# Attention beside a gated ternary feed-forward: the second score pass shifted by maximum plus logarithm of the sum, the first pass by groups of heads, contexts in two banks

## Chip, cores and metric

One Trainium2 chip, one core. The metric is the device time of one execution in microseconds, median of the runs. The engines are TensorE (PE), VectorE (DVE), ScalarE (ACT), GpSimd (POOL) and SyncE (SP), which here only issues DMAs.

## The reference

For each of 8 sequences of 512 tokens with 512 features:

```
xn = layernorm(x)
q, k, v = xn @ Wq.T, xn @ Wk.T, xn @ Wv.T      # 16 heads of 32, rope on q and k
scores = q k^T / sqrt(32), causal
s = softmax(scores) v, heads joined, @ Wo.T
h = gelu(bitlinear(xn, w_fc))                   # 512 -> 2048, ternary weights, a layernorm ahead
f = bitlinear(h, w_proj)                        # 2048 -> 512, a layernorm ahead
out = x + s * silu(f)
```

## The kernel before

All five engines run one program, written out by hand, with semaphores between them. One pass of `body(b)` handles one sequence; the body of the next one follows directly, and each engine executes its own instructions strictly in the order in which `body` emits them. Activations are split in a high and a low float16 part, so most products are two or three matmuls. The 512 tokens are four tiles of 128 (`NT`), the 16 heads are four groups of four (`NG`, `GH`), the 2048 hidden features are 16 chunks (`FC`).

For one sequence TensorE does, in this order: the value products and the query and key products (L414); the first tile of the output projection of the sequence before; the up projection (L539), 16 chunks, with the first two score rounds between the last chunks; then the **first score pass**; a stretch between the passes; and the **second score pass**, in whose last part it turns the tokens of the next sequence (L445).

**The first score pass** has 44 rounds (`ROUNDS`). A round is a tuple: tile of queries, first head, number of heads. It fills one of five PSUM banks (`S_BANKS`) with scores in which queries lie on partitions (L518), adds the causal mask by a matmul (L525), and then VectorE takes the maximum of each row (L1103), GpSimd turns it into a bias (L1322), and ScalarE takes the exponential with that bias and accumulates the sum of each row (L846). The rounds of the tile 0 have four heads of 128 keys ("short" rounds): there VectorE subtracts the maximum itself (L1111), ScalarE takes one exponential (L838), and VectorE sums, two rounds later (L1117). Before the change the rounds go tile 3 for all heads, tile 2 for all heads, and then four times a short round with two rounds of tile 1. A bank is given to the next round when its row sum is ready. Between the score rounds TensorE executes filler, `downs`: 36 matmuls of the late output projection (L431, tiles 1 to 3) and then the down projection by half tiles (L570, six halves of 32 matmuls, given two by two), and last the fourth tile (L579, 32 matmuls of 512 columns). `GIVEN[r]` says how many items of filler have been issued once round r is out: 20 after round 4, and 115 of 132 after the last round. ScalarE copies four finished halves away (L855), the last two stay in PSUM. VectorE also scales three tiles of output by the gate (L1036), after the rounds in `SCALED_AFTER`.

**Between the passes** VectorE splits the negated maxima in three float16 parts (L1025 to L1028), TensorE turns them (L605), VectorE copies them (L1144), and one DMA puts them into three more rows of the query stack, against three rows of ones in the key stack. TensorE meanwhile does the rest of the down projection and the sums for the second layernorm (L611, L616).

**The second score pass** computes the scores of each head again, with keys on partitions (L638, `scores(h)`), in two regions of PSUM used in turn; ScalarE takes the exponential of the 1280 causal columns (L869); GpSimd zeroes the masked blocks (L1351); and TensorE weighs the values (L669, `weigh(g, j)`), for a group of four heads at a time, while the scores of the next group are made. Everything of a context is in bank 6. The probabilities are not normalised: VectorE inverts the row sums (L1184), splits them (L1025 to L1028 again), TensorE turns them (L647), and for each group a matmul with a selector spreads the inverses over bank 7 (L664), VectorE copies them (L1202) and multiplies the context by them (L1205), ScalarE casts the product to float16 (L860) and GpSimd subtracts for the low part (L1357).

Around it VectorE computes mean and variance of the hidden features, GpSimd the power of -1/2 for it (L1340, `rstd_ready`), and VectorE the scale of the gate from that (L1177). GpSimd does the ten small steps of the next sequence's layernorm (`normalise_steps`, L1264 to L1282) between the passes; SP stores the norm (L308) and spreads it (L315).

## Time and profile before

| | |
|---|---|
| median of three runs | 1156.67 us (1156.52 to 1157.22) |
| profiled execution | 1157.77 us, its span 1156.0 us |
| PE busy | 1116.3 us, 97% of the span |
| DVE busy | 848.7 us, 73% |
| ACT busy | 791.5 us, 68% |
| POOL busy | 541.1 us, 47% |
| mean granted clock of TensorE | 0.999 |

The profile is of one execution. A matmul's duration in it is the time from its start to its end, and consecutive matmuls overlap, so the pace is read from starts: 16 matmuls of 512 columns that take 0.38 us each fill 3.66 us. Times of the trace are us from the start of the span.

### The profile page before, as it was taken

To read this page: it belongs to the slowest core of one execution; us is meant where nothing else is said; L and a number is where in the kernel's file an instruction comes from. 1 tells how busy PE (TensorE), PEld (TensorE's weight loads), DVE (VectorE), ACT (ScalarE), POOL (GpSimd) and SP (SyncE) were. 2 spreads that over 40 slices of the span, in tenths; PEclk is the share of its full clock that TensorE was granted. 3 is DMA by queue.
4 is the path that set the end of the run, shared out by engine and by line. 5 is a ranking of instruction groups with operands and counts; after the bars stand their busy time and mean duration, and the time that the engine had idled before them with its cause. 6 is when DMAs were issued, how large, how long until landed. Compare 5 with 4: busy or idle time off the path is not lost.

```text
span 1156.0 us, 20105 instructions
## 1 busy us (share of the span) xinstructions
PE 1116.3 (97%) x7580; PEld 609.3 (53%) x7580; DVE 848.7 (73%) x1451; ACT 791.5 (68%) x1508; POOL 541.1 (47%) x950
## 2 busy tenths in 40 slices
PE   4989999999999999999999999999999999999997
PEld 3555644448444574446644475445844467444753
DVE  6997867788457885588756886579845888558854
ACT  4787975589735878279772797448883697827974
POOL 2035352473625635275442755257362563527534
PEclk9999999999999999999999999999999999999999
DMA  8491011730109101361016411082011910145111
GB/s 309 156 108 41 1 30 37 93 88 23 30 8 145 49 3 29 44 121 37 4 28 77 88 38 30 1 107 85 11 30 23 142 38 3 28 58 71 37 40 37
DMA packets 52586, 67.31 MB, mean 58 GB/s; under 512 B 9352, under 2 KB 34312, under 8 KB 51976
## 3 DMA queue, kind: packets, MB, share of 16 engines
q1 hardware_dynamic: 52488, 66.02, 30.2%
q8 instruction: 60, 0.98, 0.4%
q14 instruction: 38, 0.31, 0.1%
HBM read 31.98 MB, written 8.40 MB: 35 GB/s over the span
## 4 chain that ended last, share of the span: by engine, by line
PE 83%; ACT 8%; DVE 5%; DMA 2%; issue 1%; SPq 1%; DVEq 0%; ACTq 0%
PE banks L414 21%; PE banks L539 17%; PE banks L570 13%; PE banks L518 5%; PE banks L669 5%; PE banks L638 5%; PE banks L431 5%; PE banks L579 4%; ACT arena L869 4%; PE banks L525 2%; ACT banks L846 1%; PE banks L445 1%; ACT split_buf L792 1%; DMA stacks<-split_buf 1%; PE banks L452 1%
## 5 line engine op out<-in xcount | busy, mean ns | idle before, releaser
L846 ACT ACTIVATE banks<-banks,mix,scl 128x512 f32<-128x512 f32 (+2 forms) x384 | 248.5, 660 | 7.2 <-POOL mix L1322 4.5
L1103 DVE TENSOR_REDUCE mix<-banks 128x1 f32<-128x384 f32 (+3 forms) x352 | 217.2, 637 | 31.0 <-PE banks L525 20.1
L539 PE MATMUL banks<-xT,fcT 128*128 128x512 f16 x1024 | 228.1, 379 | 4.6 <-ACT xh_buf L815 4.4
L570 PE MATMUL banks<-proj_ones,arena 128*128 128x256 f16 (+1 forms) x1536 | 213.3, 273 | 0.0
L869 ACT ACTIVATE arena<-banks,scl 128x1280 f32<-128x1280 f32 x128 | 164.8, 1328 | 65.4 <-PE banks L638 61.9
L1308 POOL TENSOR_TENSOR split_buf<-xr_buf,split_buf 128x512 f16<-128x512 f32 x64 | 74.0, 1177 | 254.0 <-ACT split_buf L792 254.0
L1317 POOL TENSOR_TENSOR xh_buf<-xh_buf 128x512 f32<-128x512 f32 x120 | 152.4, 1270 | 48.2 <-ACT xh_buf L815 40.2
L414 PE MATMUL banks<-xT,qkT 128*128 128x512 f16 x768 | 168.7, 379 | 0.0
L539 PEld LDWEIGHTS banks<-xT,fcT 128*128 128x128 f16 x1024 | 98.5, 98 | 124.3 <-ACT xh_buf L815 9.8
L570 PEld LDWEIGHTS banks<-proj_ones,arena 128*128 128x128 f16 x1536 | 142.6, 97 | 33.8
L1322 POOL TENSOR_SCALAR mix<-mix,scl 128x1 f32<-128x1 f32 (+1 forms) x288 | 75.9, 265 | 150.7 <-DVE mix L1103 150.1
L1076 DVE TENSOR_TENSOR arena<-banks,mix 128x512 f32<-128x512 f32 x128 | 79.5, 683 | 85.0 <-PE banks L414 85.0
L820 ACT ACTIVATE banks<-banks,scl 128x512 f32<-128x512 f32 x128 | 84.8, 663 | 75.4 <-PE banks L539 75.2
L1351 POOL TENSOR_SCALAR_AFFINE_SELECT arena<-arena 128x256 f32<-128x256 f32 x256 | 105.2, 437 | 62.3 <-ACT arena L869 62.1
L518 PE MATMUL banks<-stacks 96*128 96x128 f16 (+3 forms) x512 | 127.7, 300 | 1.5 <-DVE mix L1117 0.6
L414 PEld LDWEIGHTS banks<-xT,qkT 128*128 128x128 f16 x768 | 74.8, 98 | 87.9
L792 ACT CAST split_buf<-xr_buf 128x512 f16<-128x512 f32 x64 | 37.6, 616 | 118.9 <-DVE xr_buf L1082 78.3
L1125 DVE TENSOR_SCALAR arena<-banks,scl 128x512 f16<-128x512 f32 x128 | 96.0, 750 | 29.4 <-ACT banks L820 29.3
L1127 DVE SCALAR_TENSOR_TENSOR arena<-banks,scl,arena 128x512 f16<-128x512 f32 x128 | 96.2, 751 | 4.5
L638 PE MATMUL banks<-stacks 99*128 99x512 f16 (+3 forms) x512 | 91.4, 301 | 5.5 <-ACT arena L869 3.5
L815 ACT ACTIVATE xh_buf<-banks,scl 128x512 f32<-128x512 f32 x128 | 87.2, 681 | 0.5 <-DVE arena L1127 0.4
L669 PE MATMUL banks<-arena,v_sb 128*32 128x512 f32 (+3 forms) x1024 | 87.2, 441 | 0.0
(160 smaller groups left out, 1515.0 us busy)
## 6 DMA issues: line engine op xcount, KB each, us to landing
stacks<-split_buf SPq DMA_DIRECT2D x192, 128.0 KB, 5.1
out_dram<-arena SPq DMA_DIRECT2D x32, 256.0 KB, 2.0
xr_buf<-in_L_attn_x_dram SPq DMA_DIRECT2D x7, 1024.0 KB, 7.6
resid<-in_L_attn_x_dram SPq DMA_DIRECT2D x28, 256.0 KB, 5.3
stacks<-in_L_ffn_w_fc_dram SPq DMA_DIRECT2D x1, 4096.0 KB, 25.3
arena<-in_L_ffn_w_proj_dram SPq DMA_DIRECT2D x1, 4096.0 KB, 14.9
mix<-norm_row SPq DMA_DIRECT2D x8, 256.0 KB, 5.0
xr_buf<-in_L_attn_x_dram SPq DMA_DIRECT2D x4, 256.0 KB, 3.6
```

What stands on the lines that cost most here:

```text
L414: mm = pe.matmul(out_ap, lhs, rhs, start=(c == 0 and k == 0), stop=(c == n - 1 and k == 2))
L518: pe.matmul(bank[:, k * keys:(k + 1) * keys], q_stack[0:KS, h0 + k, i * P:(i + 1) * P], k_stack[0:KS, h0 + k, 0:keys], start=(k == 0), sto ...
L539: mm = pe.matmul(banks[:, UP_BANKS[f % NUB], :], fcT[:, c, f * P:(f + 1) * P], xT[:, part, c, :], start=(c == 0 and part == 0), stop=(c == ...
L570: mm = pe.matmul(banks[:, DOWN_BANKS[h % 3], 0:cols.stop - cols.start], hid[:, part, f, t * P:(t + 1) * P], proj_ones[:, f, cols], start=( ...
L638: mm = pe.matmul(ps[:, at:at + n], k_stack[0:KM, h, j * P:(j + 1) * P], q_stack[0:KM, h, j * P:S], start=True, stop=True)
L669: mm = pe.matmul(banks[k * DK:(k + 1) * DK, 6, j * P:S], v_sb[:, j, head * DK:(head + 1) * DK], probs[:, g % 2, k, at:at + n], start=(j == ...
L846: mm = nc.scalar.activation(block, block, ACT.Exp, scale=col(EXP_SCALE), bias=exp_bias[:, i, h0 + k:h0 + k + 1], accum_out=row_sum[:, i, h ...
L869: nc.scalar.activation(probs[:, g % 2, h % GH, :], st_region[h % 2][:, 0:PROBS], ACT.Exp, scale=col(EXP_SCALE)).then_inc(probs_ready, 1)
L1103: nc.vector.tensor_reduce(row_max[:, i, h0:h0 + n], scores_of(r), AX_X, ALU.max).then_inc(max_ready, 1)
L1127: nc.vector.scalar_tensor_tensor(hid[:, 1, f, :], up, col(INV_G), hid[:, 0, f, :], ALU.mult, ALU.subtract).then_inc(hid_lo_ready, 1)
L1317: nc.gpsimd.tensor_tensor(sq_sum[:], sq_sum[:], squares[f % NSQ], ALU.add).then_inc(sq_added, 1)
L1351: nc.gpsimd.affine_select(blocks, blocks, [[0, 2], [1, P]], ALU.is_ge, 0.0, base=0, channel_multiplier=-1).then_inc(probs_masked, 1)
```

## The change

The softmax of the second pass is normalised by its shift: the rows that are added to the query stack hold maximum + log(sum)/scale (LSE) instead of the negated maximum, against rows of minus ones. So the inversion of the sums, its split, its turn, the spread matmuls, the copies of the spread and the product with it go. The logarithm is made from the bits of the sum (one VectorE instruction), one exponential on ScalarE, and twelve small VectorE instructions. It is made for eight heads at a time: so that the first eight are done early, the rounds of the first pass now go by group of four heads (four rounds of tile 3, the short round, four of tile 2, two of tile 1), and the turned rows reach the query stack in two halves and two DMAs. The first half's logarithm stands on VectorE behind rounds 24 and 27 to 30, its turn on TensorE behind round 34. The banks of the rounds follow a list that is no longer periodic from round 25 on. All six halves of the down projection are given before the end of the rounds (`GIVEN`: 20 after round 4, then 22, 25, 28, 31, 34, ...; 79, 83, 86, 89, 92, 94, 97, 100, 102, 104, 107 after rounds 25 to 35; 132 after the last) and all six are copied away by ScalarE; of the fourth tile's 32 matmuls 16 instead of 12 are issued beside the exponentials of the second pass. Contexts of even groups are in bank 6, of odd ones in bank 7; VectorE copies each out as the high part and subtracts for the low one, without ScalarE or GpSimd. GpSimd's layernorm steps for the next sequence are issued one behind the masks of each head, and the power of -1/2 for the gate behind the masks of head 10.

The core of the diff:

```diff
+HH = H // 2
+LN2 = 0.6931471805599453
+LOG2_CENTRE = 0.0430357
+SCALE_FLOOR = 2.0 ** -7
+GUESS_AFTER = 24
+LSE_AFTER = {27: 0, 28: 1, 29: 2, 30: 3}
+TURN_AFTER = 34
+MAX_COPY_AFTER = 35
 ROPE_SHRINK = 1.0 / 16
 LN_EPS, BIT_EPS = 1e-5, 1e-6
 MASKED = -1e30
@@ -34,16 +42,22 @@
 KEY_COLS = [0, 512, 1024, 896]
 PROBS = 1280
 
-ROUNDS = [(i, h, 1) for i in (3, 2) for h in range(H)]
-ROUNDS += [r for h in range(0, H, 4) for r in ((0, h, 4), (1, h, 2), (1, h + 2, 2))]
+ROUNDS = [r for g in range(0, H, GH) for r in [(3, h, 1) for h in range(g, g + GH)] + [(0, g, GH)]
+          + [(2, h, 1) for h in range(g, g + GH)] + [(1, g, 2), (1, g + 2, 2)]]
...
-S_BANKS = (3, 4, 0, 2, 1)
-NSB = len(S_BANKS)
+NSB = 5
+S_BANKS = 5 * (3, 4, 0, 2, 1) + (3, 0, 4, 2, 1) + (0, 3, 2, 4, 1) + 2 * (0, 2, 3, 4, 1)
...
-LN_EARLY = 6
-IN_BANK_1 = LONG.index(max(r for r in range(NR) if S_BANKS[r % NSB] == 1)) + 1
+RSTD_AFTER_HEAD = 10
...
-    return [lead[r] if r < NSB else lead[-1] + (total - lead[-1]) * EXP_COLS[r - NSB] // EXP_COLS[-1] for r in range(NR)]
+    return [lead[r] if r < NSB else lead[-1] + (total - lead[-1]) * EXP_COLS[r - NSB] // EXP_COLS[-1 - NSB] for r in range(NR)]
...
-DOWN_BESIDE_EXP = 12
+DOWN_BESIDE_EXP = (3, 3, 3, 3, 2, 2)
...
-                sp.wait_ge(maxT_ready, b + 1)
-                sp.dma_start(q_stack[KS:KM, :, :], maxT[:, :]).then_inc(max_dma, 16)
+                for half in range(2):
+                    sp.wait_ge(maxT_ready, 2 * b + half + 1)
+                    sp.dma_start(q_stack[KS:KM, HH * half:HH * (half + 1), :], maxT[:, :]).then_inc(max_dma, 16)
...
+                def turn_lse(half, bank):
+
+                    pe.wait_ge(lse_split, 2 * b + half + 1)
+                    for i in range(NT):
+                        mm = pe.transpose(banks16[0:SPLITS * HH, bank, i * P:(i + 1) * P],
+                                          max_parts[:, half, i].rearrange("p s h -> p (s h)"), ident16[:])
+                    mm.then_inc(maxT_ps, 1)
...
-                while given < ahead + DOWN_BEFORE_MAXIMA:
-                    next(downs)
-                    given += 1
-
-                pe.wait_ge(max_split, b + 1)
-                pe.wait_ge(sum_ready, b * len(LONG) + IN_BANK_1)
-                for i in range(NT):
-                    mm = pe.transpose(banks16[0:SPLITS * H, 1, i * P:(i + 1) * P],
-                                      max_parts[:, i].rearrange("p s h -> p (s h)"), ident16[:])
-                mm.then_inc(maxT_ps, 1)
-
+                    if r == TURN_AFTER:
+                        pe.wait_ge(down_kept, b * N_HALF + turned_in - 2)
+                        turn_lse(0, DOWN_BANKS[turned_in % 3])
+
+                pe.wait_ge(down_kept, b * N_HALF + N_HALF - 1)
...
-                while given < ahead + NT * DOWN_MATMULS - DOWN_BESIDE_EXP:
+                while given < ahead + NT * DOWN_MATMULS - sum(DOWN_BESIDE_EXP):
                     next(downs)
                     given += 1
-
-                pe.wait_ge(sum_ready, b * len(LONG) + len(LONG))
-                pe.wait_ge(short_summed, b * len(SHORT) + len(SHORT))
...
-                    if h == 0:
-                        pe.wait_ge(max_dma, (b + 1) * 16)
+                    if h % HH == 0:
+                        pe.wait_ge(max_dma, b * 32 + 16 * (h // HH) + 16)
+                    if h < 2:
+                        last_in_region = max(q for q in range(NR) if S_BANKS[q] // 3 == h)
+                        pe.wait_ge(sum_ready, b * len(LONG) + LONG.index(last_in_region) + 1)
                     if h == 1:
-                        pe.wait_ge(centred, b * NT + 1)
+                        pe.wait_ge(sums_read, 3 * b + 3)
...
-                            pe.wait_ge(invT_ready, b + 1)
+                            pe.wait_ge(maxT_ready, 2 * b + 2)
+                        elif g == 1:
+                            pe.wait_ge(centred, b * NT + 1)
                         else:
-                            pe.wait_ge(ctx_ready, b * NG + g)
-                    if j == 1:
-                        if g == 0:
-                            pe.wait_ge(centred, b * NT + NT)
-                        pe.matmul(banks[:, 7, :], selector[:, GH * g:GH * (g + 1), :].rearrange("p h d -> p (h d)"), invT,
-                                  start=True, stop=True).then_inc(spread_ps, 1)
+                            pe.wait_ge(ctx_lo, b * NG + g - 1)
                     at, n = KEY_COLS[j], S - j * P
                     for k in range(GH):
                         head = GH * g + k
-                        mm = pe.matmul(banks[k * DK:(k + 1) * DK, 6, j * P:S], v_sb[:, j, head * DK:(head + 1) * DK],
+                        mm = pe.matmul(banks[k * DK:(k + 1) * DK, 6 + g % 2, j * P:S], v_sb[:, j, head * DK:(head + 1) * DK],
...
-                        for _ in range(DOWN_PER_HEAD if g == 0 else 0):
-                            next(downs, None)
-                        if g == 0 and k == GH - 1:
-                            turn_inverses()
+                        for _ in range(sum(DOWN_BESIDE_EXP[GH * g + k:GH * g + k + 1])):
+                            next(downs)
+                        if g == 1 and k == 0:
+                            pe.wait_ge(sums_read, 3 * b + 3)
+                            turn_lse(1, 6)
...
+                def exp_of_guess(half):
+
+                    act.wait_ge(ln_guessed, 2 * b + half + 1)
+                    nc.scalar.activation(exp_guess[:], ln_guess[:], ACT.Exp, scale=-1.0).then_inc(guess_exp, 1)
...
+            def guess_of_lse(b, half):
+                heads = slice(HH * half, HH * (half + 1))
+                dve.wait_ge(sum_ready, b * len(LONG) + len(LONG) // 2 * (half + 1))
+                dve.wait_ge(short_summed, b * len(SHORT) + len(SHORT) // 2 * (half + 1))
+                dve.wait_ge(lse_split, 2 * b + half)
+                nc.vector.tensor_scalar(ln_guess[:], row_sum[:, :, heads].bitcast(I32), LN2 / 2 ** 23, (LOG2_CENTRE - 127) * LN2,
+                                        ALU.mult, ALU.add).then_inc(ln_guessed, 1)
+            def lse_from_guess(b, half):
+                heads = slice(HH * half, HH * (half + 1))
+                parts = max_parts[:, half]
+                one_more, rest = exp_guess, ln_rest
 
                 def step(k, ins):
+                    ins.then_inc(lse_step, 1)
+                    dve.wait_ge(lse_step, (2 * b + half) * 11 + k)
+                dve.wait_ge(guess_exp, 2 * b + half + 1)
+                step(1, nc.vector.tensor_tensor(one_more[:], exp_guess[:], row_sum[:, :, heads], ALU.mult))
+                step(2, nc.vector.tensor_scalar(one_more[:], one_more[:], -1.0, None, ALU.add))
+                step(3, nc.vector.tensor_scalar(rest[:], one_more[:], -0.25, 1.0 / 3, ALU.mult, ALU.add))
+                yield
+                step(4, nc.vector.tensor_tensor(rest[:], rest[:], one_more[:], ALU.mult))
+                step(5, nc.vector.scalar_tensor_tensor(rest[:], rest[:], -0.5, one_more[:], ALU.add, ALU.mult))
+                step(6, nc.vector.scalar_tensor_tensor(rest[:], rest[:], 1.0, one_more[:], ALU.add, ALU.mult))
+                yield
+                step(7, nc.vector.tensor_tensor(rest[:], rest[:], ln_guess[:], ALU.add))
+                step(8, nc.vector.scalar_tensor_tensor(parts[:, :, 0, :], rest[:], col(INV_EXP), row_max[:, :, heads], ALU.mult, ALU.add))
+                step(9, nc.vector.tensor_tensor(part_rest[:], row_max[:, :, heads], parts[:, :, 0, :], ALU.subtract))
+                yield
+                step(10, nc.vector.scalar_tensor_tensor(part_rest[:], rest[:], col(INV_EXP), part_rest[:], ALU.mult, ALU.add))
+                step(11, nc.vector.tensor_copy(parts[:, :, 1, :], part_rest[:]))
+                nc.vector.tensor_tensor(parts[:, :, 2, :], part_rest[:], parts[:, :, 1, :], ALU.subtract).then_inc(lse_split, 1)
+                yield
+            def keep_turned_lse(b, half):
+                dve.wait_ge(max_dma, b * 32 + 16 * half)
+                dve.wait_ge(maxT_ps, 2 * b + half + 1)
+                bank = 6 if half else DOWN_BANKS[((FIRST_GIVEN[TURN_AFTER] if b == 0 else GIVEN[TURN_AFTER] - OUT_BESIDE_SCORES) + FC - 1) // FC % 3]
+                nc.vector.tensor_copy(maxT[:, :], banks16[0:SPLITS * HH, bank, 0:S]).then_inc(maxT_ready, 1)
...
+                first_half = lse_from_guess(b, 0)
                 for r in range(EARLY, NR):
                     maxima(r)
+                    if r == GUESS_AFTER:
+                        guess_of_lse(b, 0)
+                    if r in LSE_AFTER:
+                        next(first_half)
+                    if r == MAX_COPY_AFTER:
+                        keep_turned_lse(b, 0)
                     if r in SCALED_AFTER and not first:
                         scale_by_gate(b - 1, b * 8 + 8, (SCALED_AFTER[r],))
-                dve.wait_ge(max_ready, b * NR + NR)
-                split_parts(max_parts, row_max[:], -1.0, max_step, b * 3, max_split)
                 if not last:
-                    statistics(b + 1)
-                if not first:
-                    dve.wait_ge(max_dma, b * 16)
-                dve.wait_ge(maxT_ps, b + 1)
-                nc.vector.tensor_copy(maxT[:, :], banks16[0:SPLITS * H, 1, 0:S]).then_inc(maxT_ready, 1)
+                    token_statistics(b + 1, 0)
+                    token_statistics(b + 1, 1)
+                guess_of_lse(b, 1)
...
+                keep_turned_lse(b, 1)
                 step(4, nc.vector.reciprocal(var_inv, var))
                 step(5, nc.vector.tensor_tensor(nan_if_0, var, var_inv, ALU.mult))
+                dve.wait_ge(down_ps, b * (N_HALF + 1) + N_HALF + 1)
+                centre(NT - 1, banks[:, 7, :])
+                for t in range(NT - 1):
+                    centre(t, gate[:, t, :])
...
-                    if g >= 2:
-                        dve.wait_ge(ctx_lo, b * NG + g - 1)
-                    if g >= 1:
-                        dve.wait_ge(ctx_ready, b * NG + g)
-                    dve.wait_ge(spread_ps, b * NG + g + 1)
-                    nc.vector.tensor_copy(inv_spread, banks[:, 7, :]).then_inc(spread_kept, 1)
-                    dve.wait_ge(spread_kept, b * NG + g + 1)
                     dve.wait_ge(pv_ps, b * NG + g + 1)
-                    nc.vector.tensor_tensor(ctx_f32[:, g % 2, :], banks[:, 6, :], inv_spread, ALU.mult).then_inc(ctx_ready, 1)
+                    nc.vector.tensor_copy(ctxT[:, 0, g, :], banks[:, 6 + g % 2, :]).then_inc(ctx_hi, 1)
+                    dve.wait_ge(ctx_hi, b * NG + g + 1)
+                    nc.vector.tensor_tensor(ctxT[:, 1, g, :], banks[:, 6 + g % 2, :], ctxT[:, 0, g, :], ALU.subtract).then_inc(ctx_lo, 1)
...
+                        if not last:
+                            next(steps, None)
+                        if GH * g + k == RSTD_AFTER_HEAD:
+                            pool.wait_ge(var_ready, b + 1)
+                            nc.gpsimd.tensor_tensor(ffn[:, 8, :], ffn[:, 5, :], minus_half[:], ALU.pow).then_inc(rstd_ready, 1)
```

## Rows read from the trace of the kernel before

**Rows 1.** Windows of one sequence: span, then busy (instructions) by engine, clock, DMA.
```profile
557.60:567.80 10.20, 10.20 (x107) 7.05 (x105) 8.14 (x26) 3.81 (x14) 4.17 (x9) 1.00 0.03 7
567.80:595.20 27.40, 26.91 (x231) 11.71 (x230) 13.70 (x26) 24.66 (x25) 17.06 (x40) 1.00 0.15 30
...
657.60:694.60 37.00, 37.00 (x298) 27.01 (x297) 33.31 (x59) 35.49 (x98) 18.40 (x47) 1.00 0.09 30
```
**Rows 2.** Instructions of line 605, four in each sequence: durations, first and last start.
```profile
L605 PE MATMUL banks<-ident,mix x32: 219/219/237, 150.1 to 1109.2; 128*48 128x128 f16 x32
```
**Rows 3.** Timeline of TensorE in the first pass: start, duration, instructions.
```profile
680.52 0.33 PE L518 MATMUL banks<-stacks 96*128 96x384 f16 x1
...
680.75 0.60 PE L570 MATMUL banks<-proj_ones,arena 128*128 128x257 f16 x4
681.18 0.33 PE L518 MATMUL banks<-stacks 96*128 96x384 f16 x1
...
683.17 0.39 PE L518 MATMUL banks<-stacks 96*128 96x128 f16 x4
...
684.06 0.38 PE L518 MATMUL banks<-stacks 96*128 96x256 f16 x2
...
685.05 0.38 PE L518 MATMUL banks<-stacks 96*128 96x256 f16 x2
```
**Rows 4.** Timeline between the passes: TensorE, and ScalarE's first exponential of the second pass.
```profile
563.14 0.40 PE L605 MATMUL banks<-ident,mix 128*48 128x128 f16 x4
...
564.49 3.66 PE L579 MATMUL banks<-proj_ones,arena 128*128 128x512 f16 x16
...
568.74 9.38 ACT L869 ACTIVATE arena<-banks,scl 128x1280 f32<-128x1280 f32 x7 [7.32 <-PE banks L638]
```
**Rows 5.** Timeline of the second pass: TensorE's weighing and scores, ScalarE's cast and exponentials.
```profile
580.57 1.07 PE L669 MATMUL banks<-arena,v_sb 128*32 128x512 f32 x8
581.56 0.72 PE L638 MATMUL banks<-stacks 99*128 99x512 f16 x4
582.21 0.39 PE L664 MATMUL banks<-split_buf,selector 48*128 48x512 f16 x1
582.53 0.85 PE L669 MATMUL banks<-arena,v_sb 128*32 128x384 f32 x8
...
581.20 0.60 ACT L860 CAST ctxT<-split_buf 128x512 f16<-128x512 f32 x1
581.71 3.76 ACT L869 ACTIVATE arena<-banks,scl 128x1280 f32<-128x1280 f32 x3
```
**Rows 6.** Timeline of VectorE and GpSimd: steps, maxima, shift, turned rows, context, power, masks, rope.
```profile
560.06 0.23 DVE L1026 SCALAR_TENSOR_TENSOR mix<-mix 128x64 f32<-128x64 f32 x1
...
560.32 0.20 DVE L1027 CAST mix<-mix 128x64 f16<-128x64 f32 x1
...
663.94 1.88 DVE L1103 TENSOR_REDUCE mix<-banks 128x1 f32<-128x512 f32 x3
...
684.54 0.70 DVE L1111 TENSOR_TENSOR banks<-banks,mix 128x512 f32<-128x512 f32 x1
...
563.65 0.42 DVE L1144 COPY mix<-banks 48x512 f16<-48x512 f16 x1
...
579.42 0.69 DVE L1205 TENSOR_TENSOR split_buf<-banks,split_buf 128x512 f32<-128x512 f32 x1 [1.63 <-PE banks L669]
...
567.11 1.01 POOL L1340 TENSOR_TENSOR mix<-mix,minus_half 128x4 f32<-128x4 f32 x1
...
576.83 0.77 POOL L1351 TENSOR_SCALAR_AFFINE_SELECT arena<-arena 128x256 f32<-128x256 f32 x2 [0.46 <-ACT arena L869]
...
611.00 2.48 DVE L1076 TENSOR_TENSOR arena<-banks,mix 128x512 f32<-128x512 f32 x4 [9.31 <-PE banks L414]
```
**Rows 7.** First sequence: ScalarE ends a round, TensorE starts the next one in its bank.
```profile
122.39 0.79 ACT L846 ACTIVATE banks<-banks,mix,scl 128x512 f32<-128x512 f32 x1
...
123.35 0.39 PE L518 MATMUL banks<-stacks 96*128 96x512 f16 x1
```

More of the change, by code:

```diff
@@ L7 @@
 F32 = mybir.dt.float32
+I32 = mybir.dt.int32
 F16 = mybir.dt.float16
@@ L1336, in body, with mask @@
                 steps = normalise_steps(b + 1)
[L1337 to L1346 removed]
+                def mask(g):
+                    for k in range(GH):
                         pool.wait_ge(probs_ready, b * H + GH * g + k + 1)
```

189 lines of the change are left out of this document (72 added, 117 removed).

## The prediction

> **What bounds the kernel now.** I read the busy shares first (TensorE 97%), then the windows of one sequence, then the timeline and the waits inside them, and last the waits of the whole run. One sequence takes 137.0 us: the turned maxima of line 605 start first at 150.1 and last at 1109.2, seven sequences apart [rows 2]. In the first pass TensorE is busy for 37.00 of 37.00 us, between the passes for 10.20 of 10.20, in the second pass for 26.91 of 27.40 [rows 1]. Busy TensorE is not TensorE at its pace, so I checked starts: in the first pass every matmul follows the one before at its pace, and in a steady sequence no score round waits for its bank. TensorE is therefore the bound, but ScalarE (35.49 of 37.00) and VectorE (33.31) are close behind in the first pass [rows 1]. Between the passes ScalarE idles 7.32 us, up to its first exponential at 568.74 [rows 4]: that is no loss in itself, as TensorE works through it. So what counts is what TensorE no longer does, and every wait that is put in front of it.
>
> **What TensorE no longer does.** The weighing of a group starts 0.32 us behind the spread matmul (582.21 to 582.53) [rows 5]. Four of these go: 1.28 us a sequence. The Trainium skill (TensorE: Matmul & The Clock Gate, "Back-to-back issue gap") has N/2.4 + 2.5 ns for one matmul at full clock, an estimate of 0.216 us here and 0.86 for four; the row has 0.32, since a change of operand between short chains costs a little, and I take the row. By the page the total would be some 3 us higher.
>
> **What is moved between the passes.** Before, the last round is followed by 34 half-tile matmuls, then 4 + 16 matmuls of line 579, the turn, and the sums. The 34 at 0.109 us (four in 0.43: 680.75 to 681.18 [rows 3]) are 3.7 us that now stand inside the first pass, with a turn that takes about 0.4 (its row, [rows 4]). TensorE's own time in that pass becomes 37.0 + 3.7 + 0.4 = 41.1 us, and the stretch behind it is as much shorter. Moving costs and gains nothing while TensorE never waits. Four matmuls of 0.217 us (16 of them in 3.66, the last one's end included) leave the stretch for the second pass [rows 4]: 0.87 us earlier start.
>
> **The second pass.** I schedule it from its first score, S. TensorE needs 0.65 us for the scores of a head (581.56 to 582.21), 0.99 for weighing j = 0, 0.79 for j = 1 (its 0.85 less what it overlaps with the next scores) and as much for j = 2 and 3 together [rows 5]; a group takes 4 x 0.65 + 2.57 = 5.2 us, against 5.5 before. ScalarE's exponentials follow at 1.22 us (three in 3.76), 4.9 a group. Two groups of heads with 16 filler matmuls (before 12, with waits of TensorE between them) and the second turn reach S + 11.4, as before (head 10 is at 581.56, 13.7 behind 567.8, with two heads and a weighing, 2.3, between); the casts that leave ScalarE (0.60 each, [rows 5]) are not on this path. The next two groups take 5.2 each, the rest 4.5 instead of 4.8. The pass is then 26.4 instead of 27.3. With the earlier start: a gain of 0.87 + 0.95 = 1.8, with 0.1 of latency at the turn 1.9 us a sequence.
>
> **The late context.** This is a wait that the change adds. VectorE now stands in `wait_ge(rstd_ready)` ahead of its first `finish_context(0)`, and that power is issued on GpSimd behind the masks of head 10. Weighing group 2 (bank 6) waits for context 0 to be copied and split. From the end of the exponential of head 10: masks 0.1 + 0.77, power 1.04 with its issue [rows 6], two small VectorE steps 0.5, copy 0.69 and difference 0.69 with 0.1 between them (the row of line 1205 is the nearest), 0.15 to TensorE: 4.0 to 4.1 us. TensorE reaches `weigh(2, 0)` when head 11's exponential has ended (1.3 later), head 13's scores can start (0.2) and are out (0.65): 2.2, or 2.4 if it waits for the masks of head 11. The stall is 1.7 us. Behind it in TensorE's queue are the scores of heads 14 and 15, for which ScalarE then waits, so nothing is regained: +1.7. Its bounds: 0 if context 0 is done ahead of time by an order I misread, 2.5 if the masks are slowed.
>
> **VectorE in the first pass.** New there: the guess, twelve small steps and the copy of the turned rows. A step follows the one before by 0.23 to 0.26 at 64 elements (560.06, 560.32) [rows 6]; at 32 I take 0.21: 0.2 + 2.5 + 0.42 = 3.1 us. By the sum this fits: 33.3 + 3.1 in 41.1. But it comes in lumps. Maxima follow one another by 0.60 (three in 1.88), a short round costs three such pieces [rows 6]. TensorE's pace is its own part (0.23 for 384 keys, 0.45 for a short round, 0.33 for a round of tile 1: starts of the rows less 0.109 for each of their 4, 4 and 6 matmuls of filler; 0.28 for 512 keys, with 128 columns more) plus 0.218 per item of filler [rows 3].
> Around round 26 (short; its issue is 0): TensorE would issue round 30 at 3.9, 31 at 4.6, 32 at 5.6, 36 at 9.3. VectorE: maximum 26 at 0.6, shift 1.4, maximum 27 2.0, steps 1 to 3 2.6, maximum 28 3.2, sum of 26 3.8 to 4.5, steps 4 to 6 4.4, maximum 29 5.0, steps, maximum 30 6.3, steps, maximum 31 7.5, maximum 32 8.1. Round 30 uses the bank of 26, four rounds apart, and starts at 4.7: a stall of 0.8. Round 36 uses the bank of 32. Round 31's exponentials start 0.4 behind its maximum's end, at 8.6, and four of 0.54 end at 10.7. The way from there to TensorE is 0.17 for a round of tile 3 (122.39 + 0.79 to 123.35 [rows 7]); I take 0.35 here. Round 36 starts at 11.05 instead of 9.3 + 0.8: 1.0 more. Near the start VectorE is late from the up projection, and round 9 waits for the sum of short round 4, behind maxima 5 and 6 and one scaled tile: 667.0 against 666.4, 0.6. Round 15's sum is in time. Together 2.3 us a sequence. Bounds: 0 if VectorE enters each lump with a lead, 3.5 if VectorE enters each of the two lumps 0.6 us later than I have it.
>
> **What costs nothing while covered.** Two more copies by ScalarE (0.4 each) and its two exponentials of 32 columns: it has 4 us to spare in a pass of 41.1. The second half's logarithm: ScalarE ends its sums about S - 2, VectorE then needs some 5 us (sums, two statistics, twelve steps), and the turn is asked for at S + 6; the DMA leaves at S + 7.2 and is wanted at S + 11.4. If this cover were gone, each us would go to TensorE. The next layernorm is ready at S + 16 instead of S + 1; the spread norm is then some 2 us later at VectorE, which idles 9.31 us before the next rope [rows 6]. SP's queue has only the second DMA more.
>
> **The sum.** Steady sequence: -1.9 + 1.7 + 2.3 = +2.1 us, seven times +14.7. The first sequence gives 96 filler items less tightly, ScalarE bounds it (rounds wait for it at 0.17, [rows 7]), so there moving work into the pass is a gain of some 2 to 3 us against the same stalls: -0.6. The profiled execution: 1157.8 + 14.1 = 1171.9; the median of runs lies 1.1 lower: **1171 us**.
>
> **Rivals.**
> *The lumps are absorbed, the late context stays.* Five banks give some lead: at 0.9 us a round the same bank comes up again after 4 us, and the way through VectorE, GpSimd and ScalarE takes about 3. If VectorE has a lead of 2 us, the sum is 7 x (-1.9 + 1.7) - 0.6 = -2: 1154.5.
> *Neither stall: faster.* One mechanism decides: whether TensorE ever waits behind VectorE. For it: VectorE has 4 us idle in the pass by the sum. Against: context 0 is 1.7 late by an addition of five rows. Each sequence gains 1.9: 7 x 1.9 + 2 = 15, so 1141. The kernel is faster from less than 1.9 us of stall a sequence on.
> *The late context is not seen, the lumps are:* 7 x 0.4 - 0.6 = +2: 1159.
> *The second half is late too.* If the second DMA lands after S + 11.4, scores of head 8 wait; 2 us each over the forecast is 1171 + 16 = 1187. Against it: 1 us of margin.
>
> **Chances.** Forecast 0.45; lumps absorbed 0.17; lumps only 0.10; neither stall 0.18; second half late 0.10. A run tells 0.2% (2.3 us) from no change. 1154.5 is as likely faster as the same, 1159 as likely the same as slower. Faster 0.29, same 0.11, slower 0.60. The likeliest case's own range is 1162 to 1180 (stalls of 2.7 to 5.2 us a sequence). The range that holds 8 in 10 leaves out most of the fastest and slowest cases: 1146 to 1183.
>
> **What the profile after would show.** Right: the line of `weigh` waiting once a sequence for VectorE's context difference, with VectorE idle before the gate's scale until GpSimd's power; score rounds near 30 and 36 waiting for ScalarE or for the short sum; the idle time of ScalarE between the passes near 1 us; sequences 139 us apart; no spread matmul. Wrong if TensorE's busy share is still 97% and the sequences are under 137 us apart, or if TensorE waits for `maxT_ready` or the DMA.

## The result, and the profile after

The changed kernel takes 1183.61 us (median, 1182.72 to 1183.79) against 1156.89 us before (1156.52 to 1157.22) in the same set of runs: a ratio of 1.0229, 95% interval 1.0212 to 1.0247. It is slower by 26.7 us. The forecast was 1171 us, range 1146 to 1183: the direction was right, the size was not, and the top of the range lies 0.6 us under the result. The profiled execution has a span of 1182.0 us (before 1156.0).

From here on a sequence is cut in two at events that both kernels have: its *first part* runs from the first matmul of the up projection (line 546) to S, the first score of the second pass (line 653), and its *second part* from S to the next up projection. These starts repeat within 0.02 us from one steady sequence to the next, except where the text says otherwise.

| steady sequence, us | first part | second part | together |
|---|---|---|---|
| before | 75.61 | 60.85 | 136.46 |
| after, sequences 4 and 7 | 76.77 | 62.27 | 139.04 |
| after, the other steady ones | 76.77 | 63.67 to 63.85 | 140.4 to 140.6 |

So both parts lost, and the second part by two different amounts. The forecast had about +1.3 for the first part (2.3 of stalls, less 0.97 for the earlier start), and +0.75 for the second (1.7 for the late context, less 0.95).

**The first pass.** TensorE's timeline of the changed kernel, in the sequence whose first round starts at 665.58 and whose S is 717.34; line 525 is a score round (518 in [rows 3]), the other lines its mask and filler:
```profile
693.96 0.39 PE L525 MATMUL banks<-stacks 96*128 96x128 f16 x4
...
697.05 0.33 PE L525 MATMUL banks<-stacks 96*128 96x384 f16 x1
697.22 0.22 PE L532 MATMUL banks<-mask_q,ident 128*128 128x128 bf16 x1
697.27 0.82 PE L591 MATMUL banks<-proj_ones,arena 128*128 128x256 f16 x6
698.76 0.34 PE L525 MATMUL banks<-stacks 96*128 96x384 f16 x1 [0.67 <-DVE mix L1157]
...
703.27 0.39 PE L525 MATMUL banks<-stacks 96*128 96x512 f16 x1
...
705.03 0.39 PE L525 MATMUL banks<-stacks 96*128 96x512 f16 x1 [0.66 <-ACT banks L853]
```
The first row is round 26, the rows with idle time are rounds 30 and 36. Counted from round 26 they start at 4.80 and 11.07 us (forecast 4.7 and 11.05), with 0.67 and 0.66 us of idle time ahead of them (forecast 0.8 and 1.0). VectorE in between, with the first three of the twelve small steps (lines 1046 to 1060) set among the maxima, and the sum of round 26 (line 1157) ending at 698.71, just ahead of round 30:
```profile
694.60 0.69 DVE L1143 TENSOR_REDUCE mix<-banks 128x4 f32<-128x512 f32 x1 [0.63 <-PE banks L532]
695.33 0.70 DVE L1151 TENSOR_TENSOR banks<-banks,mix 128x512 f32<-128x512 f32 x1
695.94 0.55 DVE L1143 TENSOR_REDUCE mix<-banks 128x1 f32<-128x384 f32 x1
696.40 0.18 DVE L1046 TENSOR_TENSOR mix<-mix 128x32 f32<-128x32 f32 x1
696.62 0.18 DVE L1047 TENSOR_SCALAR mix<-mix 128x32 f32<-128x32 f32 x1
696.84 0.68 DVE L1048 TENSOR_SCALAR mix<-mix 128x32 f32<-128x32 f32 x1
697.55 0.56 DVE L1143 TENSOR_REDUCE mix<-banks 128x1 f32<-128x384 f32 x1
698.03 0.68 DVE L1157 TENSOR_REDUCE mix<-banks 128x4 f32<-128x512 f32 x1
```

**Between the passes**, windows of the same sequence (columns as in [rows 1]):
```profile
707.10:717.30 10.20, 10.20 (x110) 7.46 (x108) 8.24 (x21) 7.74 (x24) 1.61 (x6) 1.00 0.01 2
717.30:744.50 27.20, 24.81 (x194) 10.47 (x193) 13.52 (x37) 21.37 (x18) 18.43 (x43) 0.94 0.06 3
```
and ScalarE's first exponential of the second pass (against [rows 4]):
```profile
718.08 1.33 ACT L876 ACTIVATE arena<-banks,scl 128x1280 f32<-128x1280 f32 x1 [2.84 <-PE banks L653]
```
TensorE is full up to S, as before, and loses 2.4 us in the 27.2 behind it; the granted clock of that window is 0.94, which no window of [rows 1] shows. ScalarE idles 2.84 us ahead of its exponentials instead of 7.32 (forecast near 1). TensorE gained nothing by that, since it had work through the longer gap as well.

**The second pass.** TensorE from head 8 on (line 653 the scores, 672 the weighing), to set beside [rows 5]:
```profile
728.50 1.42 PE L653 MATMUL banks<-stacks 99*128 99x512 f16 x8
730.31 1.06 PE L672 MATMUL banks<-arena,v_sb 128*32 128x512 f32 x8 [0.39 <-POOL arena L1373]
...
732.74 0.72 PE L653 MATMUL banks<-stacks 99*128 99x512 f16 x4
733.38 0.86 PE L672 MATMUL banks<-arena,v_sb 128*32 128x256 f32 x16
734.17 1.42 PE L653 MATMUL banks<-stacks 99*128 99x512 f16 x8
...
737.59 1.72 PE L672 MATMUL banks<-arena,v_sb 128*32 128x512 f32 x8 [2.00 <-DVE ctxT L1237]
739.24 1.25 PE L653 MATMUL banks<-stacks 99*128 99x512 f16 x4
740.42 1.25 PE L672 MATMUL banks<-arena,v_sb 128*32 128x384 f32 x8
```
`weigh(2, 0)` starts at 737.59, S + 20.25, 2.00 us after TensorE was ready. Read the durations behind it: the eight matmuls of 512 columns take 1.72 us where the same eight take 1.06 at 730.31, four scores take 1.25 and not 0.72. GpSimd and VectorE ahead of it, with the power of the gate (line 1379) behind masks, and VectorE waiting for it with the context behind in its queue:
```profile
725.81 1.49 POOL L1373 TENSOR_SCALAR_AFFINE_SELECT arena<-arena 128x256 f32<-128x256 f32 x2
727.28 1.48 POOL L1301 TENSOR_TENSOR ln<-ln,minus_half 128x4 f32<-128x4 f32 x1
...
733.46 0.77 POOL L1373 TENSOR_SCALAR_AFFINE_SELECT arena<-arena 128x256 f32<-128x256 f32 x2 [0.43 <-ACT arena L876]
734.20 1.04 POOL L1379 TENSOR_TENSOR mix<-mix,minus_half 128x4 f32<-128x4 f32 x1
```
```profile
735.27 0.35 DVE L1228 SCALAR_TENSOR_TENSOR gate_scale<-mix,scl 128x4 f32<-128x4 f32 x1 [7.42 <-POOL mix L1379]
735.66 0.34 DVE L1230 TENSOR_SCALAR gate_scale<-gate_scale,scl 128x4 f32<-128x4 f32 x1
736.03 0.69 DVE L1235 CAST ctxT<-banks 128x512 f16<-128x512 f32 x1
736.75 0.69 DVE L1237 TENSOR_TENSOR ctxT<-banks,ctxT 128x512 f16<-128x512 f32 x1
```
Over the whole run the waits say the same (us in total, times, longest):
```profile
PE banks L672 <- DVE ctxT L1237: 14.0, 7, 2.1
...
PE banks L672 <- POOL arena L1373: 4.4, 8, 1.6
```
The seven waits for the context are 2.00 us in sequences 2 to 7 and 2.06 in the last. In the first sequence `weigh(2, 0)` waits 1.63 us, and there the profile names GpSimd's masks as what came last; the other seven waits for masks are the 0.39 us ahead of `weigh(1, 0)`, in every sequence but the last.

**The granted clock.** Windows of 4.30 us from the start of `weigh(2, 0)` in sequences 2 to 5; the column after POOL's is the clock:
```profile
317.30:321.60 4.30, 4.27 (x22) 1.03 (x23) 3.17 (x6) 1.33 (x1) 1.49 (x3) 0.60 0.00 0
457.90:462.20 4.30, 4.29 (x22) 1.00 (x23) 3.15 (x6) 1.15 (x1) 1.13 (x2) 0.60 0.00 0
598.50:602.80 4.30, 4.26 (x44) 1.77 (x45) 3.44 (x7) 2.40 (x2) 1.93 (x4) 1.00 0.00 0
737.50:741.80 4.30, 4.21 (x21) 0.93 (x22) 3.23 (x6) 1.27 (x1) 1.17 (x2) 0.60 0.00 0
```
In windows placed like that in all eight sequences the mean clock is 0.60 to 0.65 in six and 1.00 in the fourth and the seventh, though TensorE idled the same 2.00 us there (in the first sequence, where the clock fell as well, it was 1.63 us, in the last 2.06). Such a mean holds time at either level: from 738.0 to 741.2 the granted clock is 0.50, half of full speed. In 4.3 us TensorE issues 43 or 44 matmuls with the full clock and 21 to 24 where it fell, and its busy time, 4.2 to 4.3 us in all rows, does not show the difference.

**The account.** The spans differ by 26.0 us. The first part adds 6 x 1.16 + 1.05 = 8.0; the second part at full clock adds 6 x 1.42 = 8.5; the lower clock adds 6.1 in four of those six; the first sequence has its first part 1.0 shorter and its second 2.6 longer, the last has 2.5 more behind its S, and the start of the kernel is 0.7 shorter: 8.0 + 8.5 + 6.1 - 1.0 + 2.6 + 2.5 - 0.7 = 26.0.

### The profile page after: what moved, and what is told of

The parts are those of the page before. It is cut to its first block, busy times and chain, and to the rows that moved or that the text cites. A ratio compares the mean times of both kernels' runs of the same rounds, so it can differ in the third digit from the quotient of the medians.

```text
span 1182.0 us, 20205 instructions
## 1 busy us (share of the span) xinstructions
PE 1116.2 (94%) x7548; PEld 607.4 (51%) x7548; DVE 859.6 (73%) x1596; ACT 791.5 (67%) x1508; POOL 506.5 (43%) x915
## 4 chain that ended last, share of the span: by engine, by line
PE 71%; DVE 11%; ACT 7%; POOL 7%; issue 2%; DMA 1%; SPq 1%; DVEq 0%; POOLq 0%; ACTq 0%
PE banks L420 20%; PE banks L546 17%; PE banks L591 9%; PE banks L672 5%; PE banks L525 4%; PE banks L437 4%; POOL arena L1373 4%; DVE mix L1143 3%; ACT banks L853 3%; PE banks L602 3%; ACT arena L876 3%; PE banks L653 2%; PE banks L532 2%; PE banks L451 1%; POOL ln L1301 1%
## 5 line engine op out<-in xcount | busy, mean ns | idle before, releaser
L853 ACT ACTIVATE banks<-banks,mix,scl 128x384 f32<-128x384 f32 (+2 forms) x384 | 248.0, 648 | 37.6 <-POOL mix L1350 34.6
L1143 DVE TENSOR_REDUCE mix<-banks 128x1 f32<-128x512 f32 (+3 forms) x352 | 216.6, 638 | 42.9 <-PE banks L532 38.7
L525 PE MATMUL banks<-stacks 96*128 96x384 f16 (+3 forms) x512 | 127.9, 300 | 13.9 <-ACT banks L853 7.0
L672 PE MATMUL banks<-arena,v_sb 128*32 128x512 f32 (+3 forms) x1024 | 92.8, 465 | 18.4 <-DVE ctxT L1237 14.0
L653 PE MATMUL banks<-stacks 99*128 99x512 f16 (+3 forms) x512 | 94.4, 309 | 0.0
```

Source lines behind the costliest of these rows:

```text
L525: pe.matmul(bank[:, k * keys:(k + 1) * keys], q_stack[0:KS, h0 + k, i * P:(i + 1) * P], k_stack[0:KS, h0 + k, 0:keys], start=(k == 0), sto ...
L653: mm = pe.matmul(ps[:, at:at + n], k_stack[0:KM, h, j * P:(j + 1) * P], q_stack[0:KM, h, j * P:S], start=True, stop=True)
L672: mm = pe.matmul(banks[k * DK:(k + 1) * DK, 6 + g % 2, j * P:S], v_sb[:, j, head * DK:(head + 1) * DK], probs[:, g % 2, k, at:at + n], sta ...
L853: mm = nc.scalar.activation(block, block, ACT.Exp, scale=col(EXP_SCALE), bias=exp_bias[:, i, h0 + k:h0 + k + 1], accum_out=row_sum[:, i, h ...
L1143: nc.vector.tensor_reduce(row_max[:, i, h0:h0 + n], scores_of(r), AX_X, ALU.max).then_inc(max_ready, 1)
```

## The experiments

All were run on one chip in each set, each beside the kernel before. "After with" means the changed kernel with only the edit shown.

| kernel | median us (range) | ratio to before, 95% interval |
|---|---|---|
| power early | 1166.06 (1165.19 to 1167.60) | 1.0081 (1.0066 to 1.0096) |
| banks in turn | 1172.07 (1171.66 to 1174.95) | 1.0137 (1.0121 to 1.0152) |
| gap filled | 1174.70 (1173.10 to 1175.43) | 1.0152 (1.0135 to 1.0169) |
| before, new order of rounds | 1159.54 (1159.05 to 1160.50) | 1.0021 (1.0012 to 1.0030) |
| GpSimd's order | 1154.87 (1154.27 to 1155.86) | 0.9983 (0.9973 to 0.9992) |
| scaled tile early | 1184.20 (1182.29 to 1184.73) | 1.0231 (1.0216 to 1.0247) |
| all three edits | 1144.06 (1143.21 to 1144.54) | 0.9889 (0.9872 to 0.9905) |
| filled, tile early | 1172.36 (1171.72 to 1172.57) | 1.0128 (1.0115 to 1.0142) |
| GpSimd's order, banks in turn | 1147.27 (1146.29 to 1151.28) | 0.9920 (0.9905 to 0.9935) |
| gap filled with five | 1174.14 (1173.02 to 1174.95) | 1.0147 (1.0132 to 1.0163) |

**1. The gate's power earlier on GpSimd.** After with:
```diff
-RSTD_AFTER_HEAD = 10
+RSTD_AFTER_HEAD = 3
```


> The changed kernel with one number changed: the power of -1/2 for the gate is issued on GpSimd behind the masks of head 3 instead of head 10. Theory (the late context costs twice: 2.0 us of TensorE waiting for the difference of context 0, and behind it about 1.6 us of matmuls at the lower clock, in five of seven steady sequences): both go, 7 x 2.0 + 5 x 1.6 = 22 us, so 1161 to 1163 us, granted clock back at 0.999, and no wait of the weighing for VectorE. Rival (the wait only covers another one, GpSimd's masks, which are slowed by the steps between them): the weighing waits for the masks instead, gain under 8 us.

Measured 1166.06, 17.5 less than after, 3 to 5 more than expected. The wait for the context is gone, but a second one came out from behind it: the power now takes its 1.01 us on GpSimd ahead of masks that `weigh(1, 0)` needs. Timeline of this kernel:
```profile
587.07 1.07 PE L672 MATMUL banks<-arena,v_sb 128*32 128x512 f32 x8 [1.41 <-POOL arena L1373]
```
Seven times 1.4 us instead of 0.39 (all waits of the line: 9.9 us, 7 times). The second part is 61.23 us in every steady sequence, and the granted clock 1.00 behind this shorter idle stretch.

**2. The banks strictly in turn.** After with:
```diff
-S_BANKS = 5 * (3, 4, 0, 2, 1) + (3, 0, 4, 2, 1) + (0, 3, 2, 4, 1) + 2 * (0, 2, 3, 4, 1)
+S_BANKS = 9 * (3, 4, 0, 2, 1)
```


> The changed kernel with the five banks of the first pass simply in turn (the list of before repeated), so that no bank comes up again after four rounds. Theory (rounds 30 and 36 wait 0.8 and 0.8 us because their banks were used four rounds before, by the short round 26 and by round 32): both waits shrink to under 0.3 us, 1.2 us a sequence, 8 to 10 us in all, 1174 us. Rival (VectorE's lump of small steps is what holds TensorE, whatever bank follows): the waits move to rounds 31 to 34 and the time stays within 3 us of 1183.6. A cost of its own: the second pass's first scores now wait for the last round's sum, which ends before they are due.

Measured 1172.07, 11.5 less than after, where 8 to 10 were expected. Every round now has the bank of the one five back, so round 30 no longer asks for that of round 26. The first part is 75.67 us, 1.10 less, and within 0.06 us of that of before; TensorE's waits behind the sum of a short round (line 1157) and behind ScalarE's exponentials (line 853) fall from 6.9 and 7.0 us in the run to 2.2 and 2.3. The first sequence accounts for the 2.2; of the 2.3, 0.22 us are left at round 36 in each of the other seven. The second part of a steady sequence is 62.25 or 63.8 as before. But the lower clock now came in four sequences and not in six: it held in the first and in the last as well, whose idle stretches were the same (1.62 and 2.06 us), and that is about 3 of the 11.5 us. The edit itself is worth some 8.

**3. Does the clock cost time, or is it only seen?** The gap ahead of `weigh(2, 0)` is filled with work whose result nobody reads. After with:
```diff
 def weigh(g, j):
+    if (g, j) == (2, 0):
+        pe.wait_ge(probs_ready, b * H + 13)
+        for _ in range(12):
+            pe.matmul(banks[:, 0, 0:224], ones16[:], projT[:, 0, 0:224], start=True, stop=True)
```


> The changed kernel with twelve matmuls of 224 columns added per sequence (1.15 us of TensorE's time, into columns of bank 0 that the scores of head 14 overwrite), ahead of the weighing of group 2, once head 12's exponential has read that bank; they fall in the wait for context 0. They compute nothing that is used. Theory (the clock falls because TensorE idles there): the wait for VectorE shrinks by what the twelve fill, the weighing behind it runs at 1.06 instead of 1.72 us, granted clock above 0.995, and the kernel gets faster although it does more: by up to 5 x 1.6 = 8 us, 1175 to 1180. Rival (the slow matmuls come from VectorE and GpSimd reading beside them): they stay slow and the time is the same or up to 8 us longer.

Measured 1174.70: 96 matmuls more, and 8.9 us less. Timeline of this kernel (line 661 the filler, 676 the weighing):
```profile
731.82 1.33 PE L661 MATMUL banks<-proj_ones,ones 128*128 128x224 f16 x12 [0.72 <-ACT arena L880]
733.09 1.06 PE L676 MATMUL banks<-arena,v_sb 128*32 128x512 f32 x8
```
The weighing begins no earlier, but takes 1.06 and not 1.72. The second part is 62.24 us in all six steady sequences, as in the two of the changed kernel where the clock had held (62.27), and the granted clock behind the wait is 1.00. So the stall costs what it lasts, and apart from that some 1.5 us of lower clock where the clock falls. The rival, that VectorE and GpSimd reading beside them make the matmuls slow, is out: VectorE is as busy beside the fast ones (3.23 us of a 4.30 us window) as beside the slow ones.

**4. The order of the rounds by itself.** Before with the new list of rounds and the GpSimd loop that follows from it; the second pass stays as it was. (The list by itself leaves the engines waiting for each other: GpSimd's loop goes through the long rounds only, and one of its splits is placed behind round 26, which the new order makes a short one.)
```diff
-ROUNDS = [(i, h, 1) for i in (3, 2) for h in range(H)]
-ROUNDS += [r for h in range(0, H, 4) for r in ((0, h, 4), (1, h, 2), (1, h + 2, 2))]
+ROUNDS = [r for g in range(0, H, GH) for r in [(3, h, 1) for h in range(g, g + GH)] + [(0, g, GH)]
+          + [(2, h, 1) for h in range(g, g + GH)] + [(1, g, 2), (1, g + 2, 2)]]
...
-SQ_SPLIT_AFTER = {20: (0, 0), 22: (0, 1), 24: (1, 0), 26: (1, 1)}
+SQ_SPLIT_AFTER = {20: (0, 0), 22: (0, 1), 24: (1, 0), 27: (1, 1)}
...
-                for r in LONG[BIAS_DVE:]:
+                for r in range(BIAS_DVE, NR):
...
```


> The kernel before with only the order of its 44 rounds changed to that by groups of heads; banks in turn, filler, negated maxima and inverse sums stay, and GpSimd's half additions and splits keep their rounds. Theory (interleaved short rounds cost little by themselves; late are the steps of the logarithm and the two banks that come up after four rounds): within 0.5 us a sequence of before, 1155 to 1161 us. Rival (the short rounds among the others are what makes VectorE late): 1 to 2 us a sequence, 1165 to 1173 us.

Measured 1159.54, 2.5 us over before. The first part grows by 0.45 us, and in the steady sequences TensorE has no wait in the first pass: the order costs this in TensorE's own pace. With the banks in turn the short rounds spread over the pass cost no more than that.

**5. GpSimd's order, mended.** The power goes ahead of all but the first head's masks, four steps of the next layernorm ahead of any, and the other steps start at head 3. After with:
```diff
-RSTD_AFTER_HEAD = 10
+RSTD_AFTER_HEAD = 0
+LN_EARLY = 4
+LN_FROM_HEAD = 3
...
 steps = normalise_steps(b + 1)
+for _ in range(0 if last else LN_EARLY):
+    next(steps)
...
-    if not last:
+    if not last and GH * g + k >= LN_FROM_HEAD:
         next(steps, None)
```


> The changed kernel with GpSimd's small work placed otherwise: four of the ten layernorm steps ahead of the first masks, where GpSimd waits 6 us for ScalarE, the power for the gate behind the masks of head 0, the other steps one a head from head 3 on. Theory (with the power behind head 3 the same 1.04 us came to lie in front of the masks that the weighing of group 1 waits for, 1.4 us a sequence): neither wait is left, from a first score to the next up projection 59.9 us instead of 61.2, so 1166.1 - 7 x 1.35 = 1156 to 1158 us. Rival (the masks themselves, at 0.77 a head beside VectorE's instructions, are late): half of that wait stays, 1160 to 1163.

Measured 1154.87. TensorE runs through the second pass without a wait; three rows of its timeline from the stretch where both stalls were:
```profile
723.53 0.86 PE L674 MATMUL banks<-arena,v_sb 128*32 128x256 f32 x16
724.32 1.53 PE L453 MATMUL banks<-ident,xh_buf 128*128 128x128 f32 x12
725.78 1.07 PE L674 MATMUL banks<-arena,v_sb 128*32 128x512 f32 x8
```
The second part is 59.75 us: 1.10 less than before, which is what the change gains there once GpSimd is no longer late, and 2.52 less than after at full clock, which is what the two waits cost (2.00 and 0.39 of idle time).

**6. A scaled tile of VectorE earlier.** The rounds behind which VectorE scales three tiles for the out projection come out of a formula, 4, 7 and 11; here they are written out, and the first is one round sooner, the others where they were. GpSimd's two half additions for that tile, whose rounds are counted from these, come one round sooner too. After with:
```diff
+SCALED_AFTER = {3: 1, 7: 2, 11: 3}
```


> The changed kernel with the first of three tiles of output scaled by VectorE behind round 3 instead of round 4, so that it does not stand behind the short round. Theory: the late output projection no longer waits for it (0.9 us a sequence now), 6 us less than the changed kernel, 1177 to 1179. Rival (VectorE is late as a whole at the start of the pass and the wait goes to round 7's maximum and round 9's bank): the same time within 2 us, 1182 to 1185.

Measured 1184.20, 5 to 7 more than expected and no less than after. Yet the first part is 76.37 us, 0.40 less, in all seven sequences. In this profile the second part is 62.24 once and 63.65 to 65.14 in the other five: the lower clock came in more sequences and once lasted longer. Whether that hid the gain was tested in the next run but one.

**7. The three edits together** (2, 5 and 6).


> All together: banks in turn, the first tile scaled behind round 3, GpSimd's steps and power as in the run before last. If the waits add up as read (banks 1.1, tile 0.8, GpSimd 2.6 to 4.2 us a sequence), a sequence takes 75.0 + 59.9 = 134.9 us against 136.46 before: 7 x 1.5 + 1 = 12 us less than before, 1144 to 1147 us. Rival (the gain of the work left out is not there, since TensorE in the second pass only keeps up with ScalarE's 1.22 us a head): 1153 to 1158.

Measured 1144.06, faster than both kernels, 13.0 us under before. First part 75.29, second 59.75: 135.04 us a sequence. Of the waits of TensorE in its first pass the steady sequences keep only one, 0.22 us at round 36; seven of these and 0.8 us in the first sequence make up this row:
```profile
PE banks L528 <- ACT banks L856: 2.3, 8, 0.8
```

**8. The tile early, with the gap filled** (3 and 6).


> The gap at weigh(2, 0) filled with twelve matmuls, as in the run with 1174.7 us, and the scaled tiles of VectorE moved to rounds 3, 7 and 11. Theory: moving the tiles takes 0.39 us from the first pass of each of seven sequences (76.37 instead of 76.76 us from the up projection to the second pass), which was hidden by a lower granted clock behind the gap. With the gap filled the clock stays and the 2.7 us show: 1172 us, all stretches from the second pass to the next up projection 62.2. Rival: the early tiles are paid for elsewhere (a later out projection, a longer attention end), so 1174 to 1176.

Measured 1172.36. All six steady second parts are 62.27 or 62.28, and the first parts 76.38: now the 0.39 us show, 2.3 in the medians. The missing gain of run 6 lay in the clock.

**9. Two of the three edits** (2 and 5).


> The new order of GpSimd and the banks strictly in turn, without the early tiles. Theory: the parts add up. From the run with the new order of GpSimd (1154.9 us) the banks in turn take seven times 1.10 us: 1147.2 us; the early tiles are then worth 3.1 us of the 1144.1 us of all three. Rival: the early tiles matter only while other stalls stand, or not at all: 1144 us.

Measured 1147.27. The parts add up; the early tile is worth the 3.2 us to run 7.

**10. A shorter filling**, five matmuls in place of twelve.


> As the run with the gap at weigh(2, 0) filled by twelve matmuls (1174.7 us), but with five, some 0.5 us of work: TensorE then idles twice, 0.7 us ahead of them and some 0.7 us behind. Theory: the lower granted clock follows the long unbroken idle stretch, so with two short ones it stays at full speed: 1174 to 1175 us. Rival: what counts is how much of the gap is idle, more or less in one piece; then several sequences show the lower clock again and the time lies between, 1177 to 1182 us.

Measured 1174.14, and the second part 62.24 or 62.25 in all six. Its timeline (line 1241 is the context's difference):
```profile
730.28 0.66 PE L661 MATMUL banks<-proj_ones,ones 128*128 128x224 f16 x5 [0.72 <-ACT arena L880]
731.55 1.06 PE L676 MATMUL banks<-arena,v_sb 128*32 128x512 f32 x8 [0.61 <-DVE ctxT L1241]
```
TensorE idles 1.33 us in two pieces and keeps its clock. With one piece of 1.6 to 2.1 us it lost it in six of eight sequences (four of eight in run 2, seven of eight in run 6). The run does not settle whether the length of a piece counts or the sum: run 1 has 1.41 us in one piece, about as much, and keeps its clock too.

## Why the prediction was wrong, point by point

The step that failed is the price of a wait: the sum has every stall at its own length, and what a stall does to TensorE's clock stands in it at nothing, without a reason. That is 8.9 of the 12.6 us between forecast and result (run 3). The late context, taken at 1.7 us a sequence and measured at 2.5, is the second miss; smaller terms made up for a part of it.

- **Spread matmuls gone, second pass shorter, earlier start.** Right. The second pass alone was to gain 0.95 us and gains 1.10 (59.75 against 60.85, run 5). Gone with them is a wait of TensorE for ScalarE, 0.44 us in each sequence of before, 6.4 us behind S. The earlier start was not measured by itself; its 0.97 us fits the sum of the first part in the next point.
- **Stalls of the first pass.** Right in place; too large in size, and something else was left out. Rounds 30 and 36 start at 4.80 and 11.07 (forecast 4.7 and 11.05), but with 0.67 and 0.66 us of idle time, not 0.8 and 1.0: TensorE's own way from round 26 to 36 takes 9.7 us and not 9.3. Run 2 shows the cause of these two: with the banks in turn 1.10 us go, and 0.22 stay. The third stall was to be 0.6 behind round 9; the trace has 0.21 us, seven times, ahead of an output-projection matmul (line 437) behind a scaled tile of VectorE, and run 6 took 0.40 a sequence there, so the place was right and the releaser partly another. Together 1.7 us against 2.3 in the sum (whose own terms 0.8, 1.0 and 0.6 make 2.4). The new order of the rounds, at nothing in the sum, costs 0.45 by itself (run 4). So the first part is -0.97 for the earlier start, 0.45 for the order, 1.32 at the two banks and 0.40 at the tile, 1.20 in all; measured 1.16, forecast about 1.3. That these agree is luck in part: smaller stalls made up for the order.
- **The late context.** The term that was sized wrong. The mechanism was right: VectorE stands at the gate's power, and `weigh(2, 0)` starts 4.2 us behind the end of head 10's exponential (733.39 to 737.59; forecast 4.0 to 4.1), with TensorE ready 2.2 us behind it (forecast 2.2 to 2.4). But the term was 1.7 us, and it measured 2.5 at full clock: 2.00 for the context, 0.39 for masks of GpSimd late at `weigh(1, 0)`, and some 0.1. The 0.39 I had left out: one pair of masks takes 1.49 us and a layernorm power 1.48 from 725.8 to 728.8, where [rows 6] have 0.77 and 1.01 for such work, and three instructions of VectorE's line 1217 run beside them up to 727.85. The layernorm steps between the masks have a part in it: in the last sequence, which has none, a pair of masks takes 1.60 us at the same place and TensorE does not wait. "2.5 if the masks are slowed" stood as the bound.
- **What a stall does to the clock.** Not in the sum at all. Every stall was priced at its own length. Behind the wait at `weigh(2, 0)` the granted clock fell to the lower of its two levels, 1.2 GHz, in six sequences of eight, and each of those lost 1.2 to 1.6 us more. Of the spans, 6.1 us of it stand in four steady sequences, 1.2 in the first (second part 65.41, in run 3 64.24), 1.6 in the last (44.50 us behind its S, in run 3 42.92). Run 3 took 8.9 us off by giving TensorE more to do, which settles that the clock is a cause and not a sign. Runs 8 and 10 say the same.
- **What was covered.** Right: the scores of head 8 start at 728.50, S + 11.2, without a wait for the turned rows; the later layernorm delays nothing that TensorE waits for.
- **The first sequence.** Its first part gained 1.0; its second lost 2.56, of it 1.2 by the clock. Forecast -0.6 in all, measured +1.6, or +0.9 with the start of the kernel, which differs by up to 2.7 us between the profiles of these kernels.
- **The last sequence** was counted among the seven steady ones, at +2.1; it lost 1.05 in its first part and 2.5 behind its S, where the same wait and the lower clock stand too.

With the sizes as measured but the clock kept, the sum would have been that of run 3, 1174.7: inside the likeliest case's own range of 1162 to 1180. The 8.9 us to 1183.6 are the clock. Of the rivals, "lumps only" (1159) was run 5, 1154.9: 4 us lower, as the first part lost 1.15 instead of 1.3, the second gained 1.10 instead of 0.95, and the first sequence gained 1.9 instead of 0.6. "Neither stall" (1141) was runs 9 and 7, 1147.3 and 1144.1, with the order's 0.45 and the last 0.22 at round 36 still in each sequence. That the second half of the logarithm comes late was not seen.

What stays open: why the clock held in the fourth and the seventh sequence behind the same 2.00 us. In run 2, with the same waits, it held in the first, the second, the fifth and the eighth; in run 6 it held in the second alone. So the length of the wait alone does not decide it. No run was made to settle what does.

## What to carry to other kernels

On a TensorE-bound kernel, price a new wait at more than its length: after it, compare the duration of one matmul group with the same group elsewhere and read the granted clock in a window of a few us, because the busy share shows neither. Before adding work to an engine that serves others in order, list what stands behind each of its instructions: here one power of 128 x 4 elements, placed behind masks, held up 2 us of TensorE, and moving it alone only uncovered the next wait in the same queue. When an order of work changes, the list that hands out buffers must be redone with it: two banks reused after four rounds instead of five cost 1.1 us in each sequence.

## What the runs showed that I had not expected

- An idle stretch of 2.00 us (1.63 in the first sequence, 2.06 in the last) in an otherwise full TensorE was followed by a granted clock of 0.60 to 0.65 over 4.3 us in six of eight sequences (eight matmuls of 512 columns 1.72 us, not 1.06), and by the full clock in two; in run 2 by the full clock in four. Stretches of 1.41 us (run 1), and of 0.72 and 0.61 with 0.5 us of work between them (run 10), were followed by the full clock each time. The Trainium skill (TensorE: Matmul & The Clock Gate, "Part 1: The HAM clock gate") has two levels, 1.2 and 2.4 GHz, and a clock that follows how busy the array was. The trace agrees with the levels, the granted clock of 738.0 to 741.2 being 0.50, and run 3 with the second half, as the clock stayed full once the gap was filled.
- Matmuls that compute nothing made the kernel 8.9 us faster.
- A small VectorE step can take nearly four times its usual time: line 1048 took 0.68 us on 32 elements in the first half's logarithm, in all eight sequences, and 0.18 in the second half's. Each time it took 0.68, an addition of GpSimd (line 1363, 0.67 us) ran beside it and the two ended together; beside the short ones ran nothing of GpSimd. No run moved that addition to prove it.
- GpSimd's times go with what VectorE does beside it: the same pair of masks took 0.77, 0.95 and 1.49 us, the same power 1.01 to 1.48. Of the 256 masks of the changed kernel 226 took 0.40 to 0.44 us and 30 took 0.59 to 0.85, and all 30 ran beside one of two VectorE lines, 1217 (16 of them) and 1087 (14). That is a coincidence in the trace and not yet a test.
